# Attention plus FFN on one core: FFN2 passes between V products and scores, a start on two DMA queues, and a first FFN1 burst one pair later

## What is computed

```python
def attn(x):                       # q = k = v = the heads of x
    w = einsum('bhqd,bhkd->bhqk', q, k) / sqrt(hd)
    w = softmax(where(causal, w, min), axis=-1)
    return einsum('bhqk,bhkd->bhqd', w, v)          # back to B, S, D

def ffn(x, W1, b1, W2, b2, scale):
    lt = x[:, 1:17]; even = lt[:, ::2]; odd = lt[:, 1::2]
    m1 = (even[:, :4, :, None] * odd[:, :4, None, :]).reshape(B, H, D)
    m2 = (even[:, 4:, :, None] * odd[:, 4:, None, :]).reshape(B, D, H)
    h = gelu(x @ (W1 + scale*m1).T + b1)             # weights differ by batch
    return h @ (W2 + scale*m2).T + b2

xn = layernorm(x)
out = x + attn(xn) + ffn(xn, W1, b1, W2, b2, scale)
```

## Time and profile before

| | us |
|---|---|
| median of 3 runs (lowest, highest) | 894.2 (893.68, 894.57) |
| the profiled execution's own time | 894.16 |
| its span | 892.4 |
| PE busy | 833.6 (93%) |
| ACT busy | 686.0 (77%) |
| DVE busy | 662.3 (74%) |

### The profile page before, as it was taken

One profiled execution on the slowest core, in us unless ns is written; L12 is line 12 of the kernel. 1 busy time (PEld: TensorE's weight loads), 2 busy tenths in 40 slices (PEclk: granted clock), 3 DMA queues, 4 the chain that ended last, 5 costly groups with the idle time before them and its releaser, 6 DMA issues.

```text
span 892.4 us, 16213 instructions
## 1 busy us (share of the span) xinstructions
PE 833.6 (93%) x6272; PEld 431.7 (48%) x6272; DVE 662.3 (74%) x1356; ACT 686.0 (77%) x737; POOL 256.7 (29%) x520
## 2 busy tenths in 40 slices
PE   1579999999999999999999999999999999999997
PEld 1154644545454554545545464454545445454543
DVE  7787698867978579775997679786797868973242
ACT  0458788887887878888788878888788787888874
POOL 1213233131432314233241324313143231412211
PEclk9999999999999999999999999999999999999999
DMA  4967437391665816465173834739165561712202
GB/s 167 222 178 152 122 123 175 88 161 71 177 166 80 193 38 172 135 112 161 71 166 108 155 118 138 180 78 173 50 183 161 85 188 61 163 27 49 59 1 36
DMA packets 187053, 110.22 MB, mean 124 GB/s; under 512 B 138785, under 2 KB 155233, under 8 KB 185953
## 3 DMA queue, kind: packets, MB, share of 16 engines
q1 hardware_dynamic: 186976, 109.18, 51.3%
HBM read 75.53 MB, written 33.62 MB: 122 GB/s over the span
## 4 chain that ended last, share of the span: by engine, by line
PE 86%; ACT 8%; DVE 3%; DMA 2%; SPq 1%; issue 0%; DVEq 0%
PE o_ps L437 26%; PE work L465 22%; PE work L452 20%; PE scores L417 16%; ACT probs L370 4%; ACT L370 2%; PE work L479 1%; ACT gelu L384 1%; DMA even<-even_dram 1%; DMA xn<-x 1%; DVE w_lo L582 1%; DVE xt_w L615 1%; DMA q_dram<-xt_pair 1%; DVE w L600 0%; DVE w_hi L579 0%
## 5 line engine op out<-in xcount | busy, mean ns | idle before, releaser
L370 ACT ACTIVATE probs<-scores 128x1024 f32<-128x1024 f32 x576 | 556.7, 1024 | 145.0 <-PE scores L417 144.8
L362 POOL TENSOR_SCALAR_AFFINE_SELECT probs<-probs 128x256 f32<-128x256 f32 x512 | 254.1, 518 | 624.3 <-ACT probs L370 621.6
L437 PE MATMUL o_ps<-probs,v_ones 128*32 128x512 f32 (+3 forms) x3072 | 279.4, 493 | 0.0
L417 PE MATMUL scores<-q_stack,k_stack 64*128 64x512 f16 (+3 forms) x1536 | 181.8, 330 | 34.3 <-ACT probs L370 22.8
L437 PEld LDWEIGHTS o_ps<-probs,v_ones 128*32 128x32 f32 x3072 | 83.9, 109 | 136.6 <-issue 126.7
L417 PEld LDWEIGHTS scores<-q_stack,k_stack 64*128 64x128 f16 x1536 | 53.4, 94 | 189.1 <-ACT probs L370 136.1
L452 PE MATMUL work<-xt_hi,w_hi 128*128 128x512 f32 x256 | 104.1, 407 | 3.6 <-DVE gelu L659 3.6
L465 PE MATMUL work<-g_hi,w_hi 128*128 128x512 f32 x256 | 106.0, 414 | 0.0
L465 PE MATMUL work<-g_lo,w_hi 128*128 128x512 f32 x256 | 105.0, 410 | 0.0
L465 PE MATMUL work<-g_hi,w_lo 128*128 128x512 f32 x256 | 103.8, 406 | 0.0
L452 PE MATMUL work<-xt_hi,w_lo 128*128 128x512 f32 x256 | 100.4, 392 | 0.0
(11 more groups left out here) (44 smaller groups left out, 645.9 us busy)
## 6 DMA issues: line engine op xcount, KB each, us to landing
q_dram<-xt_pair SPq DMA_DIRECT2D x32, 512.0 KB, 4.6
q_stack<-q_dram SPq DMA_DIRECT2D x64, 256.0 KB, 4.1
k_stack<-k_dram SPq DMA_DIRECT2D x128, 128.0 KB, 4.0
xn<-x SPq DMA_DIRECT2D x16, 512.0 KB, 5.1
w<-w1t SPq DMA_DIRECT2D x8, 1024.0 KB, 7.2
k_dram<-xt_pair SPq DMA_DIRECT2D x16, 512.0 KB, 3.6
even<-even_dram SPq DMA_DIRECT2D x8, 1024.0 KB, 4.7
xt_w<-w2t SPq DMA_DIRECT2D x8, 1024.0 KB, 6.5
```

The source lines that it names most:

```text
L362: pool.affine_select(out=blk, in_=blk, compare_op=ALU.is_ge, fill=0.0, base=0, pattern=[[0, 2], [1, P]], channel_multiplier=-1).then_inc(m ...
L370: act.activation(probs[:, slot % RING, 2 * half:2 * half + 2, :].rearrange("p h q -> p (h q)"), scores[:, half, :], ACT.Exp, scale=EXP_SCA ...
L417: last = pe.matmul(scores[:, half, h * BANK + at:h * BANK + at + n], k_stack[rows, g % 2, half, kb * P:(kb + 1) * P], q_stack[rows, g % 2, ...
L437: last = pe.matmul(o_ps[VW * j:VW * (j + 1), half, q0 % BANK:q0 % BANK + n], v_ones[:, kb, heads_of(g).start + 2 * j, :], probs[:, slot % ...
```

## The change

The first part concerns every batch. A second table, `BETWEEN`, puts six FFN2 passes of the new half between the V products and the second scores of the pair behind each burst (p = 2 and p = 11); the pairs after that have six, five or four passes behind them where they had seven or five. FFN2 now waits for the split of each gelu block, and for the halves of W2, one by one. The second part concerns batch 0: the burst of pair 1 moves to pair 2 and its FFN2 passes a pair back; x is loaded in quarters by SP and ACT; the constants and the residual `acc` are loaded by ACT; q's second part and half of group 0's operands go through ACT; V is copied by ACT; the other eight heads are stored ahead of group 1's operands; and DVE does `add_m2`, `add_b2`, `evac_o` of slot 3 and the first half of `split_m2` in pairs 0 and 1.

```diff
+BETWEEN = {
+    2: [("ffn2", 0, 0, 0, 6)],
+    11: [("ffn2", 1, 0, 0, 6)],
+}
 BEHIND = {
...
-    2: [("ffn2", 0, 0, 0, 7)],
-    3: [("ffn2", 0, 0, 7, 14)],
+    2: [("ffn2", 0, 0, 6, 12)],
+    3: [("ffn2", 0, 0, 12, 18)],
...
-    8: [("ffn2", 0, 1, 14, 19), ("xn", 2)],
-    9: [("ffn2", 0, 1, 19, 24), ("xn", 3)],
+    8: [("ffn2", 0, 1, 16, 20), ("xn", 2)],
+    9: [("ffn2", 0, 1, 20, 24), ("xn", 3)],
...
+FIRST_BETWEEN = {**BETWEEN, 2: [], 3: [("ffn2", 0, 0, 0, 6)]}
+FIRST_BEHIND = {
+    **BEHIND,
+    0: [],
+    1: [],
+    2: [("ffn1", 0, 0, MT)],
+    3: [("ffn2", 0, 0, 6, 12)],
+    4: [("ffn2", 0, 0, 12, 18)],
+    5: [("ffn2", 0, 0, 18, 24)],
+    6: [("ffn2", 0, 1, 0, 6), ("xn", 0)],
...
+            x_quarter(sp, 0, 0)
+            x_quarter(sp, 0, 2)
             load_w1()
-            sp.wait_ge(xn_ready, 1)
+            sp.wait_ge(xn_half_ready, 1)
             store_even(0)
-            store_heads(0, 0)
-            load_stacks(0, 0)
+            store_k(0, 0)
+            q_part(sp, 0, 0, 0)
+            sp.wait_ge(pair_out[0], 16 * STORE_DMAS)
+            stacks_half(sp, 0, 0, 0)
             load_even(0)
+            store_heads(0, 1)
             load_stacks(0, 1)
             sp.wait_ge(xt_split, 1)
             load_w2()
-            load_acc(0)
-            store_heads(0, 1)
...
+            x_quarter(act, 0, 1)
+            x_quarter(act, 0, 3)
+            act.dma_start(scale_sb[:, :], scale.partition_broadcast(P)).then_inc(consts_in, 16)
+            act.dma_start(b1_sb[:, :], b1).then_inc(b1_in, 16)
+            for j in range(QUARTERS):
+                act.dma_start(b2_sb[VW * j:VW * (j + 1), :, :],
+                              b2.rearrange("(t j c) -> j t c", t=DT, j=QUARTERS)[j].partition_broadcast(VW))\
+                   .then_inc(consts_in, 16)
+                acc_quarter(act, 0, j)
+            act.wait_ge(xn_ready, 1)
+            act.wait_ge(v_ones_made, 1)
+            copy_v(0)
+            act.wait_ge(pair_ready, 1)
+            q_part(act, 0, 0, 1)
+            copy_v(1)
+            act.wait_ge(pair_out[0], 16 * STORE_DMAS)
+            stacks_half(act, 0, 0, 1)
...
+                    if t == 0 and n % 3 == 0:
+                        pe.wait_ge(g_split, MT * (2 * b + c) + m + 1)
+                    if t == 0 and n == FFN2_PASSES // 2:
+                        pe.wait_ge(w2_ready, 2 * b + 2)
...
+                    for what, of, *arg in between(b, p):
+                        ffn2(of, *arg)
                     if slot + 3 < ALL:
                         scores_of(slot + 3)
...
+                    if b == 0 and p == 0:
+                        add_m2(0)
+                    if b == 0 and p == 1:
+                        for t in range(DT):
+                            add_b2(0, t)
```

More of the change, by code:

```diff
@@ L105, in early_before, with work_of, between, behind @@
     return sum(EARLY) * b + sum(EARLY[:c])
-def work_of(b, p):
-    for what, *arg in (BEHIND if b else FIRST)[p]:
+def work_of(table, b, p):
+    for what, *arg in table.get(p, ()):
         if what != "xn" or b + 1 < B:
             yield what, b + (what == "xn"), *arg
+def between(b, p):
+    return work_of(BETWEEN if b else FIRST_BETWEEN, b, p)
+def behind(b, p):
+    return work_of(BEHIND if b else FIRST_BEHIND, b, p)
 def heads_of(g):
@@ L127, in _uses @@
         for p in range(PAIRS):
-            for what, of, *key in work_of(b, p):
+            for what, of, *key in (*between(b, p), *behind(b, p)):
                 if what == "ffn1":
@@ L212, in attention_ffn @@
         ident_zero, ident_made, v_ones_made = sem("ident_zero"), sem("ident_made"), sem("v_ones_made")
-        x_in = [sem("x_in0"), sem("x_in1")]
+        x_in = [sem(f"x_in{i}") for i in range(4)]
         acc_in, w1_in, w2_in = sem("acc_in"), sem("w1_in"), sem("w2_in")
@@ L229, in attention_ffn, with x_quarter, acc_quarter, q_part @@
         block = ctx.enter_context(nc.Block())
+        def x_quarter(eng, b, i):
+            blocks = slice(NT // 4 * i, NT // 4 * (i + 1))
+            eng.dma_start(xn[:, blocks, :], x[b, :, :].rearrange("(t p) d -> p t d", p=P)[:, blocks, :])\
+               .then_inc(x_in[i], 16)
+        def acc_quarter(eng, b, j):
+            eng.dma_start(acc[VW * j:VW * (j + 1), b % 2, :, :, :],
+                          x[b, :, :].rearrange("(a r) (t j c) -> j r t a c", r=VW, t=DT, j=QUARTERS)[j]).then_inc(acc_in, 16)
+        def q_part(eng, b, t, part):
+            heads = slice(HEADS // DT * t, HEADS // DT * (t + 1))
+            eng.dma_start(q_dram[b, heads, :, :, part, :].rearrange("h c a s -> (h c) a s"),
+                          xt_pair[:, part, t, :].unsqueeze(1).broadcast_to([P, 2, S])).then_inc(pair_out[t], 16)
+        def stacks_half(eng, b, g, h):
+            rows = slice(HEAD_ROWS * h, HEAD_ROWS * (h + 1))
+            eng.dma_start(q_stack[rows, g % 2, :, :],
+                          q_dram[b, heads_of(g), :, :, :, :].rearrange("(u h) c a e s -> h (c a e) u s", h=2)[h])\
+               .then_inc(stacks_in[g % 2], 16)
+            for u in range(GH // 2):
+                eng.dma_start(k_stack[rows, g % 2, u, :],
+                              k_dram[b, heads_of(g), :, :, :].rearrange("(u h) c a s -> u h (c a) s", h=2)[u, h]
+                              .unsqueeze(1).broadcast_to([2 * HD, 2, S])).then_inc(stacks_in[g % 2], 16)
         @block.sync
@@ L233, in load_x @@
             def load_x(b):
[L234 to L237, removed]
+                for i in range(4):
+                    x_quarter(sp, b, i)
             def load_acc(b):
                 for j in range(QUARTERS):
-                    sp.dma_start(acc[VW * j:VW * (j + 1), b % 2, :, :, :],
-                                 x[b, :, :].rearrange("(a r) (t j c) -> j r t a c", r=VW, t=DT, j=QUARTERS)[j])\
-                      .then_inc(acc_in, 16)
+                    acc_quarter(sp, b, j)
             def store_acc(b, half, t):
@@ L270, in store_heads @@
                              xt_pair[:, :, t, :]).then_inc(pair_out[t], 16)
+            def store_heads(b, t):
+                store_k(b, t)
                 for part in range(2):
[L272 to L273 removed]
+                    q_part(sp, b, t, part)
             def load_stacks(b, g):
@@ L496, in _ @@
                         times_v(slot + 1)
+                    for what, of, *arg in between(b, p):
+                        ffn2(of, *arg)
                     if slot + 3 < ALL:
                         scores_of(slot + 3)
-                    for what, of, *arg in work_of(b, p):
+                    for what, of, *arg in behind(b, p):
                         if what == "ffn1":
@@ L693, in _ @@
             split_m1()
-            add_m2(0)
-            split_m2(0)
-            split_m2(1)
             for b in range(B):
@@ L711, in _ @@
                         split_m2(0)
-                    if p not in BURSTS and not end:
+                    if b == 0 and p == 0:
[3 more added lines that the diff above has]
+                            add_b2(0, t)
+                    if p not in bursts(b) and not end:
                         evac_slots()
-                    if p == SPLIT_M2[1] and b:
-                        split_m2(1)
-                    for what, of, *arg in work_of(b, p):
+                    if p == SPLIT_M2[1] and b or (b, p) == (0, 1):
+                        split_m2(1 if b else 0)
+                    for what, of, *arg in behind(b, p):
                         if what == "ffn1":
@@ L726, in _ @@
                                 split_pair(of, 0)
[L727 to L730, removed]
+                    if b == 0 and p == bursts(b)[0]:
+                        split_m2(1)
+                    if p in bursts(b) or end:
                         evac_slots()
                     if more:
-                        if p == BURSTS[1]:
+                        if p == bursts(b)[1]:
                             split_pair(b + 1, 1)
```

54 lines of the change are left out of this document (21 added, 33 removed), and 11 rows, old and new, of tables (BEHIND, FIRST_BEHIND).

## The result

The changed kernel takes 887.22 us (median of 4 runs, 886.85 to 887.31) beside 894.38 for the kernel before on the same chip: a ratio of 0.9917, 95% interval 0.9902 to 0.9933. The prediction was 884.4 with a range of 879.5 to 889.0. The profiled execution took 886.85, its span is 885.1; before, the span was 892.4. So 7.3 us were gained where 9.8 were forecast.

A forecast was written before the change was run, and what follows sets the result against it. PE was taken to bound the kernel (86% of the chain), with gains where it waits for ACT and in the start. From 894.16 us, 11.4 gained in the steady part and 1.6 lost at the start gave 884.4, range 879.5 to 889.0.

The forecast's parts named there:

- The steady part: All batches: six FFN2 passes fill PE's wait for ACT behind each burst and relieve other pairs; 11.4 us gained.
- the floor of 4.61: Pairs not behind a burst: ACT sets at least 4.61 us (2.23 + 1.95 + 0.43), whatever PE has left.
- the rival without it: Pairs with six passes bound by PE, each falling by 0.244 instead of 0.14: 876.9 us, chance 0.04.
- The start: Batch 0: PE resumes the burst 3.9 us later, 4.1 is regained, 1.8 lost waiting; 1.6 lost in sum.
- the later burst: Batch 0, from PE resuming the first burst to pair 10's V products: 45.8 us instead of 49.95, 4.1 less.
- the new wait: Pair 5 of batch 0: PE waits 1.8 us for the o_ps half that DVE frees behind the next layernorm.
- the sum of the landings: Batch 0's start: even rows land at 30.1, then stores 4.1, operands 4.7 and W2 3.4 put W2 at 42.3.
- the 2.05: Group 0's operand loads: three issued on each of two queues instead of six on SP save 2.05 us.
- W2 in time: Batch 0's start: the stores ahead of W2 cost it nothing, PE resumes at 50.5; 880.2 us, chance 0.17.
- The second queue gaining nothing: Group 0's operands: transfer, not issuing, set the 4.11 us, so even rows come 2.05 later; 886.5 us, chance 0.11.
- blocked by its own DMAs: Start: the residual's loads hold ACT for twice the full-queue row, everything behind some 12 us late; 896.4 us, chance 0.03.
- Passes that don't fill the stall: Pair behind each burst: passes wait for DVE, pair takes 7.7 us, 0.76 lost per burst; some 907, chance 0.02.

The follow-up runs named there:

- one queue: The changed kernel with all six operand loads of the first group on SP's queue again: 888.04 us, ratio 0.9915.
- W2 first: The changed kernel with the other heads' stores queued behind group 1's operands and W2 instead of ahead of them: 881.6 us, ratio 0.9842.
- three passes: The changed kernel with three FFN2 passes instead of six between V products and scores behind each burst, nine behind those scores: 894.0 us, ratio 0.9992.
- the old order elsewhere: The changed kernel's start and its order in batch 0's first half, with the old FFN2 order everywhere else: 898.33 us, ratio 1.003.
- the new tables alone: The kernel before with the new FFN2 order in all batches, its start left as it was: 883.46 us, ratio 0.9862.
- no pass between: The changed kernel with no FFN2 pass between V products and scores behind each burst, all twelve behind the scores: 905.13 us, ratio 1.0111.
- the later layernorm: The changed kernel with the next layernorm's three DVE steps one pair later in batch 0 alone: 885.46 us, ratio 0.9888.
- all three edits: The changed kernel with W2 ahead of the other heads' stores, add_b2 in DVE's idle time, batch 0's layernorm a pair later: 878.4 us, 878.34 when repeated.

## Why the prediction was right, and by how much it was off

**The steady part** was right in mechanism and nearly in size: 10.9 measured, 11.4 forecast. The pair behind a burst takes 6.19 (6.17 forecast), the pairs that lose a pass fall to the floor of 4.61 and no lower, and none of the new waits for the splits shows. Of the 0.5 that are missing, 0.3 lie in batches 1 to 6: a whole batch gains 1.49 instead of 1.54 (105.64 to 104.15 between V products), as the pair behind a burst takes 0.02 more than forecast and the first burst some 0.03 more than before. The other 0.2 lie in the last batch, most of them behind its last V products (7.88 to the span's end before, 8.04 after). The floor, by which a pass less gives back only 0.14, is borne out by every pair of six passes; the rival without it would have shown pairs under 4.6.

**The start** was right in direction and too cheap, 3.6 instead of 1.6, and nearly all of that is in one number: PE goes on at 56.56 where I had 54.7. From there to pair 10's V products it is 104.25 - 56.56 = 47.7; the forecast's 45.8 and 1.8 for the wait on `o_ps` make 47.6. The terms for the later burst and for the new wait were thus right; the wait was 1.57 in the profile, and taking its cause away gave back 1.4.

The failed step is the sum of the landings: W2 landed at 44.16, not 42.3. The even rows' load was issued 2.64 earlier (23.82 against 26.46 in the earlier trace rows), nearly as forecast, but it took longer than the 6.42 of before. The view of its line says:

```profile
DMA to landing us min/median/max: 7.0/7.0/7.0
```

So the even rows landed near 30.8, not 30.1, and DVE began on them at 31.36; what held it for the other 0.5 no row shows. What issuing had given, the transfers took back in part. I had added the 2.05 at full value and kept the flight time. Then W2 landed 13.3 behind the even rows' landing instead of 12.2; the stores ahead of it, for which I took 4.1, cost 4.9 when they were moved away. The rates in that sum are those of whole stretches; in the last two of the earlier trace rows the residual's loads, issued from 31.71 on the earlier trace rows, were under way as well, so they price no single load. How the 1.9 is shared between the two terms differs from profile to profile: in the second one of the changed kernel the even rows took 7.7 and W2 landed at 43.9. SP's timeline shows what the load of W2 stood behind:

```profile
23.82 0.58 SPq L318 DMA_DIRECT2D even<-even_dram  x1
24.45 0.55 SPq L323 DMA_DIRECT2D k_dram<-xt_pair  x1
25.04 1.28 SPq L275 DMA_DIRECT2D q_dram<-xt_pair  x2
...
30.82 0.98 SPq L311 DMA_DIRECT2D xt_w<-w2t  x1
```

It landed 13.34 after its issue. With one queue it was issued 1.96 later (32.78) and landed only 0.84 later, which speaks for the transfers and against SP's issuing as what sets W2's landing; no run separates the two further. The rule that I weighed in the prediction (the Trainium skill, "DMA: Bandwidth & Descriptors", section "Issuing engines are not separate DMA queues") has a second issuing engine save issue time and nothing else. These runs agree: 2.00 of issue time were saved ahead of the even rows, and no landing gained more than that. The prediction's error was to carry the 2.05 undiminished through to W2.

**The rivals.** W2 in time is refuted by DVE's 4.81 of waiting; the kernel with W2 first shows what it would have been, 881.6 (880.2 forecast for it). The second queue gaining nothing was forecast to give 886.5 and is nearest in time, but that is luck: the even rows did come earlier by the second queue, and what the forecast lacked is spread over both landings. ACT was not blocked by its own DMAs, as its timeline shows: the last residual load was issued by 13.5 us, and ACT's store of q went out ahead of SP's last one, which is issued at 16.60.

```profile
12.90 0.59 ACTq L270 DMA_DIRECT2D acc<-x  x1
...
15.94 0.61 ACTq L275 DMA_DIRECT2D q_dram<-xt_pair  x1
```

Passes that don't fill the stall were forecast to make the pair 7.7 long; it took 6.19, and 7.37 where all twelve passes were put behind the scores.

**One thing was missing from both sums**: the first burst's 9.98 held the low clock already, before the change and after it. PE's row at the end of the gap before, and the view of stretches (0.55 is the granted clock):

```profile
50.80 0.80 PE L452 MATMUL work<-xt_hi,w_hi 128*128 128x512 f32 x1 [3.60 <-DVE gelu L659]
```

```profile
50.00:52.00 2.00, 1.21 (x3) 1.02 (x4) 1.34 (x3) 1.23 (x2) 0.00 (x0) 0.55 1.01 298
```

So it cancelled in the forecast, but a shorter gap was worth more than its length: 5.7 for 4.2 of earlier resumption with W2 first.

## What to carry to other kernels

Fill a wait with work at the place in the order where the engine stands still: with the same twelve passes in the pair the kernel took 887 us with six of them in the gap and 905 with none. Sort the loads and stores of a start by when each is wanted: here three stores queued ahead of W2 delayed its landing by 4.9 us, and loads on the other queue beside the even rows cost them less, 7.0 to 7.7 from issue to landing where they took 6.6 with one queue. When an edit moves a burst, list what else the helping engine does just behind it (here the layernorm and `add_b2`), and move that too.

## What the runs showed of the hardware that was not expected

- The last 36 matmuls of the first burst took 8.6 us where PE had stood still ahead of them for 2.46, 1.66, 0.39 or 0.38 us, all at a granted clock of 1.00. In every profile with a longer gap part of them ran at 0.50. They took 9.9 to 10.2 us behind gaps of 3.60 (the kernel before), 4.55 (three passes), 5.07 and 5.51 (the changed kernel twice) and 5.09 (the old order elsewhere), and 10.9 to 11.1 behind 4.57 (the new tables alone), 5.69 (no pass between), 5.80 (the later layernorm) and 6.69 (one queue). So a longer gap did not always cost more.
- The clock did not fall at the same point of the gap. In the two profiles of the changed kernel the mean of 52 to 54 us was 0.75 in the one and 1.00 in the other; behind the gap of 4.55 the burst began at full speed (a first matmul of 0.50 us, as with W2 first) and fell to 0.50 while it ran.
- The same 1 MB of even rows took 6.42 from issue to landing before, 6.6 with one queue, 7.0 and 7.7 in the changed kernel's two profiles, 7.09 with W2 first and 8.69 with all three edits, where `add_m1` started at 32.78 instead of 31.36 and the kernel was still the fastest. What made it longer there is open.
